# Attention, experts and attention again on one core: two elementwise products of the first stage made by GpSimd

## What is computed

```
x = x + xattn0(layernorm(x), ctx)     # bidirectional attention, W_l over [c, c2q, c*c2q, c*q2c]
x = x + ffn0(layernorm(x))            # 8 experts, 2 chosen per row, plus a shared expert
x = x + xattn1(layernorm(x), ctx)     # 16 heads
x = x + ffn1(layernorm(x))            # relu
```

```
s       = (c @ w_c + b_c)[:, :, None] + (q @ w_q + b_q)[:, None, :] + cq
a       = softmax(s, axis=2)
c2q_att = einsum('bcq,bqd->bcd', a, q)                # the attended rows
b_att   = softmax(max(s, axis=2), axis=1)
q2c_att = einsum('bc,bcd->bd', b_att, c)[:, None, :]
z       = concat([c, c2q_att, c * c2q_att, c * q2c_att]) @ W_l.T + b_l
logits  = xf @ gate_w + gate_b                        # top 2 of 8 experts for each row
shared  = gelu(xf @ ws1 + bs1) @ ws2 + bs2
```

## Time and profile before

| | |
|---|---|
| median of 3 runs | 1287.81 us |
| span of the profiled execution | 1303.4 us |
| busy in that span: TensorE (PE), weight loads (PEld) | 1239.4 us (95%), 1117.8 us (86%) |
| VectorE (DVE), ScalarE (ACT), GpSimd (POOL) | 998.1 us (77%), 813.5 us (62%), 512.1 us (39%) |
| mean granted TensorE clock | 0.982 of full speed |

### The profile page before, as it was taken

The page is one execution under the profiler, slowest core; times in us unless marked ns, Lnnn a source line. Parts: engine busy times, 40 slices in busy tenths (PEclk is TensorE's granted clock), DMA queues, the critical chain, the costliest instruction groups (busy, mean ns, idle before and its releaser), DMA issues.

```text
span 1303.4 us, 44045 instructions
## 1 busy us (share of the span) xinstructions
PE 1239.4 (95%) x17244; PEld 1117.8 (86%) x17245; DVE 998.1 (77%) x2454; ACT 813.5 (62%) x1552; POOL 512.1 (39%) x553
## 2 busy tenths in 40 slices
PE   6899999984999999998899999999999999999997
PEld 5788888874999999996688888888888888888886
DVE  4888888875555555536988898889888988898884
ACT  4477766642655555565567666766676667666753
POOL 2466666654121212135544344424442444343010
PEclk9899999997899999998899999999999999999999
DMA  3124333112422222213101110111011101110000
GB/s 110 64 80 147 96 122 82 64 68 71 134 82 72 80 72 80 73 53 76 33 16 34 35 33 16 34 34 29 21 35 34 33 16 34 34 33 12 11 11 18
DMA packets 86536, 71.21 MB, mean 55 GB/s; under 512 B 25088, under 2 KB 73216, under 8 KB 86368
## 3 DMA queue, kind: packets, MB, share of 16 engines
q1 hardware_dynamic: 74768, 42.71, 11.4%
q0 software_dynamic: 11600, 26.10, 6.5%
HBM read 40.73 MB, written 28.05 MB: 53 GB/s over the span
## 4 chain that ended last, share of the span: by engine, by line
PE 83%; DVE 10%; issue 3%; POOL 1%; ACT 1%; DMA 1%; another core or an unknown queue 0%; SPq 0%; DVEq 0%; POOLq 0%; ACTq 0%
PE c_ps_w L84 23%; PE d_ps_y L1218 10%; PE c_ps_w L1731 8%; PE d_ps_h L84 8%; PE c_ps_s L1697 5%; PE c_ps_w L1720 4%; PE c_ps_w L1706 4%; PE c_ps_w L1748 4%; PE a_ps_w L84 3%; PE a_ps_w L917 2%; PE a_ps_w L872 2%; PE a_ps_w L825 1%; PE d_ps_x L1197 1%; PE c_ps_w L1603 1%; DVE a_a_diag L670 1%
## 5 line engine op out<-in xcount | busy, mean ns | idle before, releaser
L1484 POOL DMA_INDIRECT c_back<-sorted_y,k_y_row_of x112 | 112.8, 1007 | 177.8 <-PE c_ps_w L1720 144.8
L93 POOL DMA_INDIRECT sorted_x<-a_xn,f_slot_of x128 | 127.9, 999 | 84.5 <-PE a_ps_w L917 36.6
L1218 PE MATMUL d_ps_y<-e_w_all,d_h_t 128*128 x1136 | 139.1, 276 | 0.0
L1083 POOL DMA_DIRECT2D sorted_y<-d_y_rows x71 | 50.8, 716 | 213.0 <-DVE d_y_rows L1114 208.8
L1218 PEld LDWEIGHTS d_ps_y<-e_w_all,d_h_t 128*128 128x128 f32 x1136 | 134.0, 193 | 0.0
L1731 PEld LDWEIGHTS c_ps_w<-c_wo,c_o_t 128*128 128x128 f32 x1024 | 122.5, 192 | 5.6 <-ACT c_o_t L1945 1.4
L1731 PE MATMUL c_ps_w<-c_wo,c_o_t 128*128 128x128 f32 x1024 | 124.9, 275 | 0.9 <-ACT c_o_t L1945 0.6
L1945 ACT COPY c_o_t<-c_ps_w 128x512 f32<-128x512 f32 x128 | 68.8, 590 | 78.4 <-PE c_ps_w L1720 78.4
L1510 POOL TENSOR_TENSOR c_rstd<-c_var,c_minus_half 128x1 f32<-128x1 f32 x64 | 35.7, 558 | 200.0 <-DVE c_var L2135 200.0
L1166 ACT ACTIVATE d_h_t<-d_ps_h,d_biases 128x256 f32<-128x256 f32 x284 | 111.7, 475 | 2.5 <-PE d_ps_h L84 2.1
L2152 DVE TENSOR_TENSOR c_shifted<-c_ps_s,c_mask 128x1024 f32<-128x1024 f32 x64 | 78.0, 1219 | 41.7 <-PE c_ps_s L1697 41.6
(11 more groups left out here) (264 smaller groups left out, 3596.1 us busy)
## 6 DMA issues: line engine op xcount, KB each, us to landing
d_x_rows<-sorted_x SPq DMA_DIRECT2D x71, 128.0 KB, 2.1
sorted_y<-d_y_rows POOLq DMA_DIRECT2D x71, 128.0 KB, 2.2
k_X<-in_x SPq DMA_DIRECT2D x16, 256.0 KB
a_q_rows<-in_ctx SPq DMA_DIRECT2D x16, 256.0 KB
ctx_cols<-a_q_t SPq DMA_DIRECT2D x16, 256.0 KB
k_ctx_raw<-ctx_cols SPq DMA_DIRECT2D x16, 256.0 KB, 3.9
out<-k_X SPq DMA_DIRECT2D x15, 256.0 KB, 3.1
sorted_x<-a_xn,f_slot_of POOLq DMA_INDIRECT x128
```

Of the source, the lines that this page charges most:

```text
L93: pool.indirect_dma_start(out=sorted_x, out_offset=bass.IndirectOffsetOnAxis(ap=slot_of[:, choice, t:t + 1], axis=0), in_=xn2[:, k, :], in ...
L1218: last = pe.matmul(ps_y[c % 2][:, k * D:(k + 1) * D], h_t[c % 2][:, j, k * P:(k + 1) * P], w2_all[:, ds(e * HC + j, 1), :].rearrange("p a ...
L1484: pool.indirect_dma_start(out=back[:, choice, k, :], out_offset=None, in_=sorted_y, in_offset=bass.IndirectOffsetOnAxis(ap=y_row_of[:, cho ...
```

## The change

`low_xn` and the product `cc_t` move from VectorE to GpSimd. GpSimd cannot be given the PSUM bank as operand, so `low_xn` now subtracts from `xn_t`, the copy that ScalarE makes for the gate. Three waits follow: the PSUM bank of `xt` is free once ScalarE has made both copies (`xn_high` in place of `xn_low`); ScalarE's `take_xn` waits for `xn_low` of the group before, since it overwrites `xn_t`; and `low_xn` waits for `xt_ready` too. GpSimd does `cross(a)` as the last thing of a turn and `low_xn(c)` as the first of the next.

```
@@ -248,7 +248,7 @@
-                    "xt": (xn_low, g + 1), "totals": (totals_read, 1)}[kind]
+                    "xt": (xn_high, g + 1), "totals": (totals_read, 1)}[kind]
@@ -362,6 +362,19 @@
+            def low_xn(g):
+
+                pool.wait_ge(xt_ready, g + 1)
+                pool.wait_ge(xn_high, g + 1)
+                pool.tensor_tensor(xn_s.low[:], xn_t[:], xn_s.high[:], ALU.subtract).then_inc(xn_low, 1)
+
+            def cross(g):
+
+                if g >= 1:
+                    pool.wait_ge(full, full_at("z", g - 1))
+                pool.wait_ge(c2q_ready, NB * (g + 1))
+                pool.tensor_tensor(cc_t[:], c2q_t[:], c_t[g % 2][:], ALU.mult).then_inc(cc_ready, 1)
+
@@ -373,6 +386,8 @@
             for t in range(TURNS):
                 a, b, c, d = groups_of(t)
+                if c is not None:
+                    low_xn(c)
                 if d is not None and d < G - 1:
                     scatter(d, GT, GT + 1)
@@ -404,6 +419,8 @@
                 if t + 2 < G:
                     root1(t + 2)
+                if a is not None:
+                    cross(a)
@@ -466,6 +483,7 @@
             def take_xn(g):
                 if g >= 1:
+                    act.wait_ge(xn_low, g)
                     act.wait_ge(full, full_at("up", g - 1, SC - 1))
@@ -541,10 +559,6 @@
-            def low_xn(g):
-                dve.wait_ge(xn_high, g + 1)
-                dve.tensor_tensor(xn_s.low[:], bank("xt", g)[:], xn_s.high[:], ALU.subtract).then_inc(xn_low, 1)
-
@@ -713,7 +727,6 @@
-                dve.tensor_tensor(cc_t[:], c2q_t[:], c_t[g % 2][:], ALU.mult).then_inc(cc_ready, 1)
@@ -724,7 +737,6 @@
                 if c is not None:
-                    low_xn(c)
                     slots(c)
@@ -759,8 +771,6 @@
-                if c is not None:
-                    low_xn(c)
                 if d is not None:
                     add_shared(d, 0)
```

## The result

The changed kernel takes 1318.5 us (1317.1 to 1320.2, 4 runs) against 1288.7 us for the kernel before (4 runs): 1.0231 times as long, 95% interval 1.0219 to 1.0244, or 29.8 us more. The forecast was 20.7 us more. The profiled execution of the changed kernel took 1317.06 us with a span of 1315.4.

The account below looks back on a forecast made before the run. Bound: TensorE, busy 16.73 of 17.09 us, and close beside it VectorE's gapless 6.41 us row. Full turns add 18.5 us, turns 2 and 16 together 2.2: 20.7 us on the 1287.81 median gives 1308.5, range 1299 to 1319.

Parts of the forecast that it names:

- The delay of the ranks: Between logits and maxima, two GpSimd products of 1.31 us each hold VectorE's ranks, 2.62 us in all per turn.
- Who goes first: At the ranks' start: L562 runs, `cc_t` waits for it, L563 waits for `cc_t`, `low_xn` follows, then L564 to L570.
- The slack of 0.60 us: Between VectorE's ranks and maxima: idle time of 0.63 us less 0.03 to issue absorbs 0.60 us of delay per turn.
- The leaving of `low_xn`: VectorE's unbroken row from maxima to `b_att` shrinks from 6.41 to 5.81 us, a gain of 0.60 us per turn.
- TensorE can give it: TensorE's waits of 0.24 and 0.30 us at L832 and L842 leave room for the 0.60 us gain.
- the rival of a faster kernel: Products and ranks run side by side, so 14 turns gain 0.55 us each from `low_xn`: 1281 us, chance 0.09.
- The sum over the turns: First stage, turns 3 to 15: 13 full turns, each 1.42 us longer, add 18.5 us.
- Turn 2: First turn with ranks: estimated to lose 1.1 us, as much as turn 16.
- From turn 15's maxima on: Turn 16: `z` waits 0.8 us and L562 1.2 us for the products, taken as 1.1 us; the tail left unchanged.
- TensorE's clock: Rival: with 1.8 us idle per turn, TensorE's clock could fall, adding some 15 us: 1324 us, chance 0.05.
- the forecast case: First stage: both GpSimd products fall inside VectorE's ranks, 20.7 us more, 1308.5 us, own range 1301 to 1317, chance 0.80.
- the widened range: Whole kernel: the forecast's own range of 1301 to 1317 us, widened by the tail to 1299 to 1319.

Follow-up runs that it names:

- the other profiled execution: The unchanged kernel profiled a second time: 1288.29 us, span 1286.6, turn 16.73; median of its runs 1288.3 us, ratio 0.9998.
- `cc_t` alone: Against the kernel before, only the product `cc_t` moves to GpSimd, `low_xn` stays on VectorE: 1302.8 us, ratio 1.0117.
- copies: The kernel before plus two GpSimd copies of a 128x512 tile at the end of each of the first 16 turns: 1299.0 us, ratio 1.0073.
- VectorE late by itself: The kernel before plus three unused 128x512 products on VectorE between logits and ranks in 14 turns, GpSimd untouched: 1320.8 us, ratio 1.0241.
- two products more: The kernel before plus two unused GpSimd products of 128x512 at the end of each of the first 16 turns: 1317.7 us, ratio 1.0219.
- the run without the two products: The changed kernel with `low_xn` and `cc_t` made by no engine, their tiles zeroed once at the start: 1288.9 us, ratio 1.0005.
- the low halves in the middle of the turn: Against the kernel before, only `low_xn` on GpSimd, mid-turn behind the second block's scatter, and VectorE's `norm_shift1` behind `slots`: 1292.8 us, ratio 1.0029.
- the low halves alone: Against the kernel before, only `low_xn` moves to GpSimd, where the change puts it; `cc_t` stays on VectorE: 1299.7 us, ratio 1.0081.
- both products behind scatters: The changed kernel with GpSimd's `cc_t` between group c's third and fourth scatters and `low_xn` after group d's second: 1339.8 us, ratio 1.0403.

## Why the prediction was right, and where it was off

*The direction and the mechanism* were right: GpSimd's products hold VectorE's ranks. The chain that I named follows too: sums waiting for the counts, `mrow` for the maxima.

*The delay of the ranks*, 2.62 us, was 2.41. A product takes 1.26 us there and not the 1.31 of L358.

*Who goes first* was wrong. I had L562 run, then a product, then L563, then the other product. Instead the first of the ranks waits for both and the rest are untouched, though it is recorded 0.05 us ahead of the first product. The sum doesn't depend on the order.

*The slack of 0.60 us* before the maxima, read from one turn, does not exist in the other profiled execution. The runs bound what a late VectorE gets back at 0.25 (`cc_t` alone), 0.28 (copies, VectorE late by itself) and 0.33 us (two products more).

*The leaving of `low_xn`* I priced at 0.60 us. From the maxima to the next logits the changed kernel is 0.85 us faster; with 0.30 of that for the late VectorE, 0.55 are left for `low_xn`, so the turn is 2.41 - 0.30 - 0.55 = 1.56 us longer, where I had 2.62 - 0.60 - 0.60 = 1.42. A turn breaks even at a hold of 0.85 us and not of 1.20, and each product alone costs 1.2. In a turn where VectorE isn't late, the leaving is worth nothing (the run without the two products, and the low halves in the middle of the turn): the step "TensorE can give it" failed. The 0.24 us at L832 stood in that execution alone; in the other, TensorE's `mrow` follows the sums without a wait for `low_xn`. So the rival of a faster kernel, 1281 us, had no ground even with no rank held. The overlap that I gave for it, of `root1` with `cc_t`, is 176.26 - 176.15 = 0.11 us and not 0.07.

*The sum over the turns.* Full turns: 18.5 forecast; measured 17.3 in eleven intervals and 0.8 in the last.

*Turn 2*: 1.1 forecast, 3.2 measured. Its own ranks aren't held (L576 takes 0.42 us at 39.89, and its maxima start at 42.84 in both kernels). The first held ranks are those of turn 3: from logits to maxima they take 5.70 us against 3.22, 2.48 more, and here nothing comes back, since VectorE wasn't late before them. The other 0.73 us are the logits (57.49 against 56.76), behind a `z` of turn 2 that stands at 1.2 GHz to about 49.6 us and did to 48.1. In the run with the low halves alone the logits are late by 0.5 us too and the maxima start 0.24 us sooner; with `cc_t` alone they aren't late. Why the clock rises later stays open.

*From turn 15's maxima on*: 1.1 forecast, all for turn 16; measured 2.9. In turn 16 `z` waits 0.82 us for `cc_t` (0.8 forecast) and L576 takes 1.93 us, 1.51 more (1.2 forecast), and the last queue of 15 scatters starts 1.5 us later than by the turns alone (311.98 against 285.00, less 25.5). The other 1.5 us are the product L369 that stands in that queue. I had seen it (1.3 us) and put it at nothing for ScalarE's 12.83 us of idle time; in an execution without that stall the queue of scatters is the bound.

*TensorE's clock* I held for a rival with a chance of 0.05 and 15 us; it came on top of the forecast case, for 4.1 us.

So the forecast had 18.5 + 1.1 + 1.1, and the spans say 18.2 + 3.2 + 2.9, 4.1 for the clock and 0.4 in the later stages, 28.8 in all; the medians differ by 1.0 us more than the spans. Of the 9 us that the forecast lacked, the clock is 4.1, turn 2 is 2.1 and the tail 1.8.

*Luck* had a part in both numbers. The 1.42 us of a turn are near 1.56 because errors nearly cancel: the hold was 0.21 us too long, what comes back from the slack 0.30 and the leaving of `low_xn` 0.05 too large. And 1318.5 lies 0.5 us inside the widened range and 1.5 outside the forecast case's own, with a term of 4.1 us that neither of them had.

## What to carry to other kernels

Before moving elementwise work from VectorE to GpSimd, lay GpSimd's new reads beside every VectorE instruction in the same stretch whose operands all lie on chip, here the ranks, `f_cum` and the normalisation: a product of 1.26 us that meets a rank of 0.42 holds it for 1.2 us, and with both products put under a wait for TensorE and beside PSUM reads the turn was 0.1 us longer (16.84 against 16.73). First ask what a free move would give, by leaving the work out: here it was nothing, since TensorE is busy for 16.3 of 16.7 us. And take slack from more than one profiled execution; 0.6 us of it stood in one and not in the next.

## What was not expected of the hardware

- By the records, whose spans on GpSimd are rough, a product queued directly behind another GpSimd instruction holds VectorE from before its own recorded start. In the run with both products behind scatters, the third of the normalisation's instructions began at 294.94, 0.62 us ahead of `cc_t`'s record (295.56), and took 1.98 us. The scatter that was still running doesn't do this by itself: in the second execution of the kernel before, all four take 1.12 us beside one that starts with them (L703 and L93, both at 153.99). In the changed kernel L576 is recorded 0.05 us ahead of `cc_t` and lost to it.
- Two GpSimd products in a row leave VectorE no gap, two GpSimd copies do: 2.83 us on one rank against 0.96 and 0.82 on two.
- The small powers (L348, 128x4, 1.04 us) hold next to nothing where they meet VectorE's on-chip work, which is for 0.2 us at most: in the two executions of the kernel before, `cc_t` takes 0.72 to 0.73 us with 0.10 to 0.12 us of overlap and 0.68 to 0.69 without, and L562 0.42 to 0.43 either way.
- Between the maxima of turns 3 and 15, TensorE's clock fell to 1.2 GHz only in runs whose turn at full clock is 18.3 us or more (the windows of all runs with turns up to 17.7 show 1.00 throughout). In the changed kernel the fall shown lasts from about 83.9 to 87.2 us, in the middle of `z`, with two waits of about 0.6 us before it. The same waits stand before turns without a fall (0.65 and 0.60 us at 100.86 and 102.04), so what tips it stays open. Such a fall costs 1.03 us there and 0.94 to 1.03 in three more runs. In the run with both products behind scatters the falls are longer: one lasts from about 115 to 121 us and one from about 156 to 166, each behind a wait for the normalisation (1.64 and 1.70 us).
